# A language-model tower on one core: the query's bank in the encoder, the order of the second attention, and the products of the experts

## The reference

```python
# 1: encoder, 4 layers, 16 heads of 16
y = layer_norm(h); q, k, v = y @ attn_w[l, :3] + attn_b
o = softmax(q k^T / 4) v;  h = h + o @ attn_w[l, 3] + b
y = layer_norm(h);         h = h + relu(y @ w1 + b1) @ w2 + b2
# 2: attention in windows of 128 tokens, 16 heads of 64, 16 learned keys and values ahead of each window
h = h + concat_heads(softmax(mask(q [pm_k; k]^T / 8)) [pm_v; v]) @ w_out
# 3: 16 experts, 2 of them per token, at most 320 tokens each, and 2 shared ones
logits = flat @ gate_w; topi = top_k(softmax(logits) + gate_b, 2)
out[idx] += (silu(x @ w1) * (x @ w3)) @ w2 * weight     # per expert, x = flat[idx]
out += mean over 2 shared experts of the same form
```

## Time and profile before

| | before |
|---|---|
| median of 3 runs | 2048.26 us (2046.69 to 2048.64) |
| the profiled execution, its time | 2048.48 us |
| its span in the trace | 2046.7 us |
| PE busy | 2006.4 us (98%), 16486 matmuls |
| DVE busy | 1296.1 us (63%) |
| ACT busy | 1038.8 us (51%) |
| POOL busy | 216.4 us (11%) |
| granted PE clock, mean | 0.999 |

### The profile page before, as it was taken

One profiled execution on the slowest core, in us unless ns is written; L12 is line 12 of the kernel. 1 busy time (PEld: TensorE's weight loads), 2 busy tenths in 40 slices (PEclk: granted clock), 3 DMA queues, 4 the chain that ended last, 5 costly groups with the idle time before them and its releaser, 6 DMA issues. The chain is left out here.

```text
span 2046.7 us, 42301 instructions
## 1 busy us (share of the span) xinstructions
PE 2006.4 (98%) x16486; PEld 1663.4 (81%) x16486; DVE 1296.1 (63%) x3345; ACT 1038.8 (51%) x3524; POOL 216.4 (11%) x251
## 2 busy tenths in 40 slices
PE   7999999999999999999999999999999999999998
PEld 5888888888888888888888888787788788877776
DVE  5776777777777777767767763777776646322232
ACT  4666665666666666666665562554454631111111
POOL 1111000000000000000000000000000000334444
PEclk9999999999999999999999999999999999999999
DMA  3110000200000400000000000400000100034542
GB/s 92 32 56 7 7 2 2 71 2 1 2 2 1 159 2 2 1 2 2 1 1 2 2 2 28 160 2 1 1 1 1 63 1 11 30 91 154 170 135 65
DMA packets 27203, 69.84 MB, mean 34 GB/s; under 512 B 9920, under 2 KB 17825, under 8 KB 23680
## 3 DMA queue, kind: packets, MB, share of 16 engines
q1 hardware_dynamic: 18432, 59.42, 8.6%
q0 software_dynamic: 6400, 5.63, 1.1%
q10 hardware_dynamic: 2176, 2.10, 0.3%
HBM read 61.16 MB, written 17.40 MB: 38 GB/s over the span
## 5 line engine op out<-in xcount | busy, mean ns | idle before, releaser
L576 ACT ACTIVATE probs<-bank,nmax 128x256 f32<-128x256 f32 x1024 | 471.9, 480 | 233.7 <-DVE nmax L751 233.1
L751 DVE TENSOR_REDUCE nmax<-bank 128x2 f32<-128x512 f32 x512 | 322.1, 682 | 68.1 <-PE bank L407 68.1
L420 PE MATMUL bank<-ident,probs 128*128 128x128 f32 x2048 | 273.5, 277 | 1.4 <-DVE pts L759 0.7
L420 PEld LDWEIGHTS bank<-ident,probs 128*128 128x128 f32 x2048 | 230.2, 141 | 49.6 <-issue 34.0
L452 PE MATMUL bank<-yT,weights 128*128 128x256 f32 x1024 | 238.9, 381 | 9.6 <-DVE qm L727 9.6
L585 ACT ACTIVATE pts<-bank 128x512 f32<-128x512 f32 x256 | 157.0, 613 | 153.4 <-PE bank L420 152.3
L464 PE MATMUL bank<-weights,aT 128*128 128x256 f32 x1024 | 231.7, 379 | 2.2 <-ACT probs L576 1.9
L452 PEld LDWEIGHTS bank<-yT,weights 128*128 128x128 f32 x1024 | 187.2, 190 | 37.5 <-issue 15.9
L576 ACT ACTIVATION_READ_ACCUMULATOR probs<-bank,nmax 128x1 f32 x1024 | 215.8, 211 | 0.0
L464 PEld LDWEIGHTS bank<-weights,aT 128*128 128x128 f32 x1024 | 191.9, 190 | 28.0 <-issue 2.8
L759 DVE COPY pts<-bank 128x512 f32<-128x512 f32 x256 | 175.8, 687 | 46.2 <-PE bank L420 42.3
(11 more groups left out here) (222 smaller groups left out, 2982.1 us busy)
## 6 DMA issues: line engine op xcount, KB each, us to landing
wqkv<-in_experts SPq DMA_DIRECT2D x16, 1024.0 KB, 5.1
weights<-in_wtok SPq DMA_DIRECT2D x4, 2048.0 KB, 10.4
wqkv<-in_experts SPq DMA_DIRECT2D x16, 512.0 KB, 3.7
expert_rows<-xT_all SPq DMA_DIRECT2D x10, 546.0 KB, 16.6
xrows<-expert_rows SPq DMA_DIRECT2D x16, 273.0 KB, 3.2
weights<-in_wtok SPq DMA_DIRECT2D x3, 1024.0 KB, 4.7
wqkv<-in_wqkv SPq DMA_DIRECT2D x1, 3072.0 KB, 17.8
weights<-in_shared SPq DMA_DIRECT2D x1, 3072.0 KB, 12.5
```

Source lines behind the costliest of these rows:

```text
L420: last = pe.transpose(g[:, (NT * x + kb) * P:(NT * x + kb + 1) * P], p[:, x, kb * P:(kb + 1) * P], ident[:])
L576: last = nc.scalar.activation(probs[u % 8][:, x, :], g[:, x * S:(x + 1) * S], ACT.Exp, bias=nmax[j % 2][:, col:col + 1], accum_out=rsum[j ...
L751: nc.vector.tensor_reduce(nmax[j % 2][:, col:col + 2], g[:].rearrange("p (x s) -> p x s", x=2), AX.X, ALU.max, negate=True).then_inc(s_max, 1)
```

## The change

1. Encoder: the query of the next job goes to bank 6 in place of bank 7, and `o` takes its turn on bank 6 one step later in the list (at c = 3, where its first product is computed anyway).
2. Second attention: `pts` gets a second buffer; `pv` of two groups is done together, right behind the scores, at the odd steps (groups G - 3 and G - 2), into banks 6 and 7; projections, transposes and the copies of ACT and DVE are put in a new order with new banks. At the first sequence step 0 has only two of the four value products (`v`) and no transpose of the next norm; these stand in step 1, behind the turned probabilities of group 0. 13 products of the shared experts are done early in place of 15, and LAST_X, LAST_LG and KEYS_AT keep their distance of 2, 3 and 6 slots to that number. The projection of the last sequence stands last, with no upper product behind it in the steps.
3. Experts: the two lower parts go to banks 6 and 7 and are signalled one by one (`s_down` counts 2 per expert), the 64 rows go to the right half of bank 6 once DVE has added the first part; the wait for each of the four inputs `gT` stands ahead of the product that reads it. The banks are handed over by ACT (behind `stored`), five before it copies the first rows and one behind, and the ring begins behind the bank used last.

```diff
@@ encoder, order of the banks
-                jq, cq = divmod(GROUPS * j + c - 2, GROUPS)
-                if cq == 0:
-                    use((jq, "o"), 6)
+                if c == 3:
+                    use((j, "o"), 6)
...
-                    use(ahead(j + 1, "q"), 7), use((j - 1, "y2T"), 0), use(ahead(j + 1, "k"), 1), use((j - 1, "up", 0), 7)
+                    use(ahead(j + 1, "q"), 6), use((j - 1, "y2T"), 0), use(ahead(j + 1, "k"), 1), use((j - 1, "up", 0), 7)
@@ second attention
-    EARLY = 15
-    LAST_X, LAST_LG = 17, 18
-    KEYS_AT = 21
+    EARLY = 13
+    LAST_X, LAST_LG = EARLY + 2, EARLY + 3
+    KEYS_AT = EARLY + 6
...
-        pts = sb("w_pts", [P, 9, P])
+        pts = [sb("w_pts", [P, 9, P]), weights[0][:, 4352:5504].rearrange("p (n s) -> p n s", n=9)]
@@ PE, scores(G)
+                if s and w == 0:
+                    for i in (2 * half, 2 * half + 1):
+                        evacuated(pe, ("q", s, i))
+                        evacuated(pe, ("k", s, i))
@@ PE, the new order of a step
                     if G < GR:
                         scores(G)
+                    if c % 2:
+                        for H2 in (G - 3, G - 2):
+                            if 0 <= H2 < GR:
+                                pv(H2)
                     if 1 <= G <= GR:
                         turn_probs(G - 1, 0)
                         turn_probs(G - 1, 1)
+                    ahead(s, c, "A")
                     ahead(s, c, "B")
+                    if c == 0 and 0 < s < B:
+                        project("q", s, 2)
+                        project("k", s, 2)
+                    if c == 1 and seq(s):
+                        project("v", s, 2)
+                        project("v", s, 3)
+                    if c in (2, 3) and seq(s + 1):
+                        project("q", s + 1, 0 if c == 2 else 3)
+                        project("k", s + 1, 0 if c == 2 else 3)
+                    if 1 <= G <= GR:
+                        turn_probs(G - 1, 2)
+                    ahead(s, c, "C")
+                    ahead(s, c, "D")
+                    if c == 0 and seq(s - 2):
+                        logits(s - 2)
                     if c == 0 and seq(s):
+                        project("v", s, 0)
                         project("v", s, 1)
+                    if c == 1 and seq(s - 1):
+                        project_out(s - 1, 1)
+                    if c == 1 and seq(s + 1):
+                        y_T(s + 1)
+                    if c == 2 and seq(s + 1):
+                        project("q", s + 1, 1)
+                        project("k", s + 1, 1)
                     if c == 3:
                         project_out(s, 0)
                     if c == 3 and seq(s - 1):
                         x_T(s - 1)
@@ DVE, the new order of a step
+                    if c == 0:
+                        wo_out(s - 1, 0)
+                    if c == 2:
+                        wo_out(s - 1, 1)
                     for j in range(4):
                         mask_max(G, j)
                     copy_pt(G - 1)
                     if c == 0:
+                        if s:
+                            k_out(s, 2)
+                        else:
                             normalise(1, 4)
                         normalise(s + 2, 0)
...
                     if c == 3:
+                        gate_norm(s - 1)
+                        k_out(s + 1, 3)
                         normalise(s + 2, 4)
                     norm_probs(G)
...
+                        if s == B:
+                            wo_out(B - 1, 1)
+                            choose(B - 2, 1)
@@ experts, PE, down(e)
-                for i in range(HT):
-                    evacuated(pe, (e, "up", 2 * i + 1))
                 if e:
                     pe.wait_ge(s_new, RT * e)
-                g = bank[6]
+                else:
+                    bank_left(pe, 6)
                 for i in range(FULL):
                     for k in range(HT):
-                        last = pe.matmul(g[:, i * D:(i + 1) * D], gT[a][:, k, i * P:(i + 1) * P],
+                        if i == 0:
+                            evacuated(pe, (e, "up", 2 * k + 1))
+                        last = pe.matmul(bank[6 + i][:, 0:D], gT[a][:, k, i * P:(i + 1) * P],
                                          w2[a][:, k, :], start=(k == 0), stop=(k == HT - 1))
-                last.then_inc(s_down, 1)
-                g = bank[7]
+                    last.then_inc(s_down, 1)
+                pe.wait_ge(s_new, RT * e + 1)
                 for k in range(HT):
                     for x in range(2):
-                        last = pe.matmul(g[64 * x:64 * x + 64, 0:D // 2], gT[a][:, k, FULL * P:CAP],
+                        last = pe.matmul(bank[6][64 * x:64 * x + 64, D:D + D // 2], gT[a][:, k, FULL * P:CAP],
@@ experts, ACT
+            def hand_over(n):
+                i = (first_bank + n) % 6
+                bank_left(act, i)
+                nc.scalar.activation(scratch[:, i:i + 1], half_of[:, 0:1], ACT.Copy).then_inc(s_free[i], 1)
+
+            for n in range(5):
+                hand_over(n)
             rows_out(0)
+            hand_over(5)
@@ experts, DVE
-            bank_left(dve, 6)
-            for i in range(6):
-                bank_left(dve, i)
-                nc.vector.memset(scratch[:, i:i + 1], 0.0).then_inc(s_free[i], 1)
...
-                dve.wait_ge(s_down, e + 1)
                 for i in range(FULL):
+                    dve.wait_ge(s_down, FULL * e + i + 1)
                     dve.wait_ge(s_old[i], 16 * (e + 1))
```

More of the change, by code:

```diff
@@ L985, in use, with dense @@
             order.append((u, b))
+        def dense(s, c, x, b):
+            if (s, c, x) in early:
+                use(upper(early[s, c, x]), b)
         for s in range(B + 1):
@@ L1007, in attention_and_shared @@
-                    use(("wo", s, 0), 0)
-                if 1 <= G <= GR:
-                    for part in range(3):
-                        use(("pt", G - 1, part), 4 + part % 2)
-                    use(("o", G - 1), 6)
-                if (s, c, "C") in early:
-                    use(upper(early[s, c, "C"]), 5 if seq(s) else 7)
-                if c == 0 and seq(s):
-                    use(("v", s, 2), 7 if s else 4), use(("v", s, 3), 3 if s else 5)
-                if c == 0 and (s, c, "D") in early:
-                    use(upper(early[s, c, "D"]), 3)
@@ L1187, in pv @@
                             last = pe.matmul(o[r, (n // 2) * P:(n // 2 + 1) * P], val[:, hd * DH2:(hd + 1) * DH2],
[L1188 removed]
+                                             pts[G % 2][:, n if own else 8, :], start=not own, stop=own)
                 filled(last, ("o", G))
@@ L1386, in copy_pt @@
                 n, to = (4, 4 * part) if part < 2 else (1, 8)
-                release(nc.scalar.activation(pts[:, to:to + n, :], g[:, 0:n * P].rearrange("p (n s) -> p n s", n=n), ACT.Copy), u)
+                release(nc.scalar.activation(pts[G % 2][:, to:to + n, :], g[:, 0:n * P].rearrange("p (n s) -> p n s", n=n), ACT.Copy), u)
             def o_out(G):
@@ L1841, in experts @@
             order += [(e, "up", i) for i in range(HT, 2 * HT)]
-        place = {u: (n % 6, n // 6) for n, u in enumerate(order)}
+        first_bank = (last_bank + 1) % 7 % 6
+        place = {u: ((first_bank + n) % 6, n // 6) for n, u in enumerate(order)}
         s_full = [sem(f"e_full{i}") for i in range(6)]
```

178 lines of the change are left out of this document (67 added, 111 removed).

## The result

The changed kernel takes 2027.27 us (median of 4 runs, 2026.10 to 2027.91), the kernel before, run beside it, 2048.45 us (4 runs, 2046.69 to 2048.71). The ratio is 0.9898, with a 95% interval of 0.9886 to 0.9909: 21 us less, where 20 were predicted (2028.5, range 2023 to 2037). The profiled execution took 2026.10 us, its span is 2024.3 us, and the granted clock is 0.998 on the mean.

A forecast was written before the change was run, and what follows sets the result against it. PE, busy for 98% of the span, was taken as the bound. The terms -14.1 - 7.7 - 4.2 + 5.8 + 1.3 + 0.5 - 1.4 sum to -19.8 us, giving 2028.5 us, range 2023 to 2037.

The forecast's parts named there:

- the likeliest case: Whole kernel: the forecast's own sum of gains and losses, -19.8 us to 2028.5, range 2024 to 2033, chance 0.62.
- a: Encoder: the wait moves to the copy of `y2T`, half of the 14.1 us is lost, 2035.5; chance 0.12.
- c: Encoder: VectorE's query copies hold up all of c = 2, so the encoder gives nothing, 2042.6; chance 0.04.
- b: Second attention: the new order waits about 1.1 us each sequence for a late bank, 2036; chance 0.12.
- d: Second attention: `norm_probs` at c = 3 comes late behind the key's copy, making the kernel slower, 2052; chance 0.04.
- e: Second attention: the start waits less and shape changes cost more than taken, 2022; chance 0.06.
- Encoder: Feed-forward unit `up 0` no longer waits for the query's copy: 0.47 us a job, 14.1 us less.
- Tile shapes: Second attention: fewer changes between full and small-tile matmuls, 1.03 us a sequence over 7.5 sequences, 7.7 us less.
- Waits for `w_pts`: Second attention: value products no longer wait for the copies of turned probabilities, 4.2 us less.
- First sequence: Second attention's start: new waits for group 0's probabilities (4.4) and `v` banks (0.9, 0.5), +5.8 us, bounds 4.0 and 7.5.
- End of the attention: Last projection to last rows' transposes: PE waits about 1.8 us and saves 0.51, +1.3 us, bounds 0 and 2.5.
- Experts: Experts: bank hand-over by ACT +0.5 us, middle 0, end -1.4 us (bounds 0 and 1.7).

## Why the prediction was right

**The whole.** 21.2 by the medians against 19.8, inside the likeliest case's own range. The chance lay on the case that came, and none of the rivals' mechanisms is seen: `up 0` waits for nothing (a, c), no sequence but the first waits (b, d), the first sequence lost what was forecast or nearly (e).

**Encoder: right, size too small.** The term was 0.47 a job, and a job gained 0.556. The gap was read rightly, 1.35 to 0.87, 0.48. What it left out stands in the earlier trace rows: the unit behind the wait lasts 1.97 there and 1.89 in the other step; from its first instruction to its second it takes 0.29, where the others are 0.22 apart. The 0.08 goes with the wait, and over 30 jobs that is 2.4 us. The 0.01 that I took off for caution was not needed: the slack was 0.08.

**Tile shapes: right, size a fifth too large.** The term was 1.03 a sequence. A full sequence got shorter by 1.14, of which about 0.3 is the value products' wait behind the logits, so about 0.8 is left. The step that failed is "transposes behind small tiles: 0.06": the starts show 0.12, and with four such units a sequence that makes 0.79. I had read lengths where only distances of starts count. The run with the pairs apart gives the same price by itself, 0.69 for four changes of shape, 0.17 each.

The Trainium skill (TensorEngine Tiling (Array Packing), Key Properties) says that every change of tiling mode drains the engine; with the constant of about 166 ns from its page TensorE: Matmul & The Clock Gate (Single matmul latency) the estimate was 0.83 for the five changes saved. The trace agrees with that better than with my sum: about 0.8 measured, and 0.17 a change.

**Waits for `w_pts`: right.** No wait of the value products is left. One thing was missed: in sequence 1 of the kernel before, which has no logits to do, PE waited in their stead (47.33 with and without them), so that this sequence gained 2.04 in place of 1.14; the 4.2 us of the earlier trace rows hold that wait already.

**First sequence: right in size and place, not in its form.** +5.8 was said; with 0.8 x 7.5 = 6.0 for shapes and 4.2 for waits, the measured -5.3 for the whole attention leaves about +5. That is a remainder, not a row. The forecast had PE do the scores of group 1 without a wait and then wait 3 to 5 us for the probabilities. In fact PE waited four times for the exponentials that free the banks of these scores, 2.0 us together, and then only 1.25 for the probabilities; both waits hang on the same chain, so the size held. By an estimate, the products at half the clock for 3.41 us take up to 1.7 longer, and with the waits of 3.2 that makes the 5; it is no loss on top of the chain, since without that fall the time would be a wait (35.43 and 35.46 behind the first sum, table above). PE began to turn the probabilities 10.66 behind its first scores, where the forecast had them ready at 10.2. The two waits for the banks of `v` do not appear in the changed kernel. They are seen in the run with the mask early, shorter than said (0.56 and 0.28, where 0.9 and 0.5 were forecast).

What lay behind it I had not seen: "nothing in the change makes them earlier" is true, but the chain hung on a transfer that it does not need, that of `pmv`, and 2.8 us of it can be had. I had also called a fall of the clock possible at +1.7. It came in every profile of the new order in which VectorE's first sum waited for `pmv` and PE had no idle products to do (7), and in none of those with the old order (2), the early mask (3) or idle products and no early mask (1); against a chain that PE waits for anyway it cost nothing or up to 1.3.

**End of the attention: right.** PE waits 1.74, the stretch costs 1.1. The run with one product more between shows that the wait was only a matter of distance: 1.73 came back.

**Experts.** The hand-over costs 0.6 (0.5 said). ScalarE's five activations take 0.57 together, but PE's transposes start 0.35 behind the start of the first (1793.98 to 1794.33), so that only the first, of 0.19, is on the path, where I had reckoned with one of 0.2. The tail gave 1.8, shown by the run with the old form (29.54 against 27.74); I had said 1.4 with a bound of 1.7, so the measured value is just outside. The middle gave nothing, as said. Not foreseen was a fall of the clock at the first expert, 1.7 in the profiled execution. By the rows it follows a stretch in which PE was busy for 1.29 of 3.40 us; but the same stretch with the same waits stayed at 1.00 in other runs, so no cause is shown.

**Sum.** Encoder 2.6 better (16.7 with the job of the second row), tail 0.4 and end of the attention 0.2 better; attention 0.8 worse, hand-over 0.2 worse, clock at the first expert 1.7 worse: the errors nearly cancel, and that the total came so close is partly luck. Of the 2.7 at the start of the profiled execution 2.1 are the luck of that run.

## What to carry to other kernels

Look for a bank that is asked for again by its next user before its copy is over, and give it another that has long been free: the query's bank (and the turn of `o` that makes room for it) was worth 17 of 21 us here. Where the engine is busy for 98%, the rest hides in changes of tile shape that count as busy time (0.17 us each): put blocks of one shape together and read starts, not lengths. And where a stage begins, follow the first wait back to its transfer, and ask whether the waiting instruction reads it. Two loads that count on one semaphore make the user of the small one wait for the large one: here the mask of 72 KB for `pmv` of 512 KB. A semaphore for each, or a load during the stage before, is cheap.

## What was not expected of the hardware

The granted clock went to 0.50, the lower of its two levels (1.2 GHz), for 3.41 or 6.83 us at three places: near 27 us, at the first sequence and at the first expert. Only at the first sequence did it follow the kernel: 7 profiles of 7 in which VectorE's first sum waits for `pmv` in the new order and PE has no idle products (one of them with the pairs apart), 0 of 6 otherwise. At the other two places the same instructions came with and without it, in 6 and in 4 of the 13 profiles. At the first expert it costs 1.6 to 1.7 us, more than several of the edits tried give.

Two more things differ from run to run without the kernel: PE's first scores of the encoder start at 19.9 to 21.4, and 8 of the 13 profiles have the two pauses of PE near 55 us, for which no semaphore is named. With them the second job takes 34.1 to 34.2 us in place of 33.2 in the kernels with the new encoder. Profiled spans that differ by 1 us must be compared stretch by stretch.

The landing of `pmv`, issued 0.20 behind PE's first scores in each profile without the early mask, lay 3.6 to 4.0 us behind them in most of these and 5.5 behind in two. In those two the issue of one of the next transfers took SyncE 1.5 and 2.0 us in place of 0.43; the mask, ahead of it, landed as early as ever.
